# A longer pipeline for the attention sums of a graph network: four banks and buffers, totals two steps later, work moved between three engines

## The chip, the cores and the metric

The kernel runs on one core of one Trainium2 chip. The metric is the device time of one execution in microseconds (us); it comes from unprofiled runs. One more execution was profiled, and all rows below are from it. Engines are named as in the profile: PE is TensorE (PEld its weight loads), DVE VectorE, ACT ScalarE, POOL GpSimd, SP SyncE. A "q" behind an engine's name (SPq) marks work of its sequencer: register operations, waits, DMA issues.

## The reference, cut to what matters

A graph network of four layers over 6250 nodes and 100000 edges, whose targets `dst` are sorted. Layers 0 and 2 (heads H = 8 and 4) weigh the values of the edges by a softmax over each node's incoming edges and add them up. The core of it, from layer 0:

```python
a = jnp.exp(a - amax[edge_dst])
a = a / (jax.ops.segment_sum(a, edge_dst, num_segments=n)[edge_dst] + 1e-12)
ns = jax.ops.segment_sum(vs * a[..., None], edge_dst, num_segments=n).reshape(n, H * H0)
nv = jax.ops.segment_sum(vv * a[..., None, None], edge_dst, num_segments=n).reshape(n, H * H1, 3)
```

The kernel forms the sums of value times weight and the sums of the weights in one pass and divides later. One edge has 160 values: 64 scalars (`C0`), and 32 vectors in three components (`C1` = 32 columns each).

## The kernel before

The program is a row of phases with a barrier between them. `attention_sums` (L1339) is one of them and runs twice, for layer 0 and for layer 2. It walks over V = 244 blocks of 512 edges (128 partitions by `TM` = 4): 196 blocks of the sorted list, and up to 48 visited a second time, where a block spans two windows of 128 nodes. For each block:

- **SP** reads the block's number from `W["block"]` into a register (`value_load`) and issues three loads: values `val` (320 KB), targets `key`, weights `pb`. There are `RING` = 4 buffers of each. Before the load of block i it waits until block i-4 was weighed, by the semaphores `weighted_s` (DVE's part) and `weighted_v` (POOL's part).
- **POOL** adds the window's shift to the targets (`rel`), multiplies the three vector components of `val` by the weights into `wv`, and copies the weights themselves into the last H columns of `wv`.
- **DVE** multiplies the 64 scalar columns into `wv`, and compares `rel` with the lane numbers: `hot`, a 128 by 512 one-hot matrix of 0 and 1.
- **PE** adds up the block's edges by target: four matmuls of `hot` with `wv` into the PSUM bank `psS`, 160 + H columns wide. A matmul in f32 shows as two records, so a block has eight.
- **DVE** adds the bank to the running `total` (times `keep`, which is 0 where a new window begins), and **ACT** issues its store to `sums`.

`rel`, `hot`, `wv` and `psS` have two buffers each. `steps` (L84) writes a loop with a skew: in step n an engine works on block n for skew 0 and on block n-1 for skew 1. It unrolls the first steps (`lead`), then runs a hardware loop whose turn holds four steps, then the rest. `wait_apart` is a wait on a semaphore that is a separate instruction of the engine's sequencer; inside the loop the same instruction also counts up a spare semaphore.

Nothing orders the engines but these semaphores: each engine runs its own instructions in the order written.

Of the kernel before, what the change touches and what calls it, by code (L numbers as in the profile page):

```python
# [16 lines left out]
I32 = mybir.dt.int32  # L17
# [1321 lines left out]
def attention_sums(nc, W, D, layer, H, tag):  # L1339
    HS, HV = C0 // H, C1 // H  # L1340
    width = CX + H
    sums = D["sums"][layer]
    with ExitStack() as ctx:
# [5 lines left out]
        rel, hot, wv = ring("rel", [P, TM], 2, I32), ring("hot", [P, TM, P], 2), ring("wv", [P, TM, width], 2)  # L1349
        total = ring("total", [P, width], RING)  # L1350
        psS = [S.ps(f"psS{u}", [P, 512]) for u in range(2)]
        values, weights = blocks_of(D["val"]), blocks_of(D["probs"][H])
        targets = D["dst_sorted"].rearrange("p t -> (p t)").rearrange("(m q k) -> m q k", q=P, k=TM)
        LAST = 1
        block = ctx.enter_context(nc.Block())

        @block.sync
        def _(sp):
            sp.dma_start(sums[0], W["zeros"][:, 0:width]).then_inc(sem("first"), 16)

# [14 lines left out]
        def _(pool):  # L1375
            tt = nc.gpsimd.tensor_tensor

            def body(i_of):
                if m := i_of(0):
                    i, u, j = m  # L1380
                    wait_apart(pool, sem(f"in{u}"), (j + 1) * 48, sem("pool_passed"))
                    wait_apart(pool, sem("hot"), i - 1, sem("pool_passed"))
                    tt(rel[u % 2][:, :], key[u][:, :], W["shift"][:, bass.ds(i, 1)].to_broadcast([P, TM]), ALU.add).then_inc(sem("rel"), 1)
# [10 lines left out]
        def _(dve):  # L1394
# [3 lines left out]
            def body(i_of):  # L1398
                if m := i_of(0):
                    i, u, j = m  # L1400
                    dve.wait_ge(sem(f"in{u}"), (j + 1) * 48)
                    wait(dve, sem("summed"), i - 1)
                    tt(wv[u % 2][:, :, 0:C0].rearrange("p t (h c) -> p t h c", h=H), val[u][:, :, 0:C0].rearrange("p t (h c) -> p t h c", h=H),
                       bcast(pb[u][:, :, :], 3, HS), ALU.mult).then_inc(sem("weighted_s"), 1)
                    dve.wait_ge(sem("rel"), i + 1)
                    tt(hot[u % 2][:, :, :], bcast(W["lane"][:, :], 1, TM), bcast(rel[u % 2][:, :], 2, P), ALU.is_equal).then_inc(sem("hot"), 1)
# [1277 lines left out]
```

## Time and profile before

| | |
|---|---|
| median of 3 unprofiled runs | 12669.28 us (12666.13 to 12681.18) |
| the profiled execution | 12702.04 us, its span 12700.3 us |
| `attention_sums`, layer 0: SP's first load to its last | 2983.7 to 3603.5 us of the span |
| `attention_sums`, layer 2 | 9926.4 to 10530.4 us of the span |

The two phases are about a tenth of the span. No other phase contains a line that the change touches. The page gives for each engine the busy time and the share of the span; they are averages over phases of quite different kinds, and what the change is worth has to be read inside the two stretches of the table.

### The profile page before, as it was taken

Reading aid. Unit: us, or ns where it says so; the run is one execution under the profiler, and the core shown is the slowest. Engines: PE = TensorE matmul, PEld = TensorE weight load, DVE = VectorE, ACT = ScalarE, POOL = GpSimd, SP = SyncE. Lnnn points to the kernel's source line nnn. Section 1 sums busy time; section 2 is a strip of 40 time slices with the busy share of each in tenths; the row PEclk is TensorE's granted clock in tenths of the full one; section 3 lists DMA queues with packets and bytes.
Section 4 is the critical chain, followed back from the end, with each engine's and each line's share of the span. In section 5 each row is a group of like instructions: output and inputs, shape, how many; then the busy total and the mean of one; then the engine's idle time right before and its main releaser. Section 6 shows DMA issues by size and latency. Waiting matters only on the chain. (4 is left out here: it accounts for less than half of the span.)

```text
span 12700.3 us, 220425 instructions
## 1 busy us (share of the span) xinstructions
PE 9229.7 (73%) x44798; PEld 7244.6 (57%) x44798; DVE 8713.2 (69%) x21701; ACT 4529.6 (36%) x11637; POOL 8172.7 (64%) x8692
## 2 busy tenths in 40 slices
PE   2899999973655666666664578888887465999985
PEld 2888888863545322222223477777776454565654
DVE  4677777777643555555554389999999764667763
ACT  1455555540012222222221267777776001333331
POOL 4788888864843788888882176666664582666650
PEclk7777777776865777777776589999898786899995
DMA  3455555434620688888885233333332562333331
GB/s 91 106 114 115 113 113 114 115 85 112 170 74 15 111 131 131 131 130 131 130 132 141 102 79 81 81 81 81 81 81 67 129 170 59 84 87 87 93 87 41
DMA packets 1339110, 1293.91 MB, mean 102 GB/s; under 512 B 504078, under 2 KB 1142018, under 8 KB 1338374
## 3 DMA queue, kind: packets, MB, share of 16 engines
q0 software_dynamic: 347904, 594.12, 25.6%
q1 hardware_dynamic: 913580, 653.03, 20.0%
q10 hardware_dynamic: 77530, 45.68, 1.2%
q8 instruction: 36, 0.59, 0.0%
q14 instruction: 60, 0.49, 0.0%
HBM read 781.38 MB, written 510.73 MB: 102 GB/s over the span
## 5 line engine op out<-in xcount | busy, mean ns | idle before, releaser
L664 POOL DMA_INDIRECT e_gs<-tab_src,e_ix x1568 | 1708.1, 1089 | 763.2 <-issue 429.9
L664 POOL DMA_INDIRECT e_gd<-tab_dst,e_ix x1568 | 1610.7, 1027 | 477.8 <-issue 474.4
L715 PE MATMUL e_psS<-e_rows,e_same 128*128 128x480 f32 x1568 | 1113.6, 876 | 848.2 <-DVE e_same L689 848.2
L603 PE MATMUL e_psF<-w_ident,e_F 128*128 128x128 f32 x6272 | 1293.0, 315 | 246.9 <-ACT e_F L1822 233.0
L733 POOL DMA_INDIRECT acc<-e_sums,e_row x784 | 1247.5, 1591 | 239.0 <-issue 206.7
L715 PEld LDWEIGHTS e_psS<-e_rows,e_same 128*128 128x128 f32 x1568 | 430.6, 293 | 1541.7 <-issue 1514.7
L1642 POOL DMA_INDIRECT e_g<-tab_src,e_er x976 | 970.1, 994 | 525.1 <-issue 284.1
L633 ACT ACTIVATE e_FT<-e_psF 128x384 f32<-128x384 f32 (+1 forms) x2352 | 1078.0, 458 | 538.5 <-PE e_psF L603 526.4
L1431 PE MATMUL s_psS<-s_wv,s_hot 128*128 128x168 f32 (+1 forms) x3904 | 800.0, 361 | 615.2 <-POOL s_wv L1389 242.6
L603 PEld LDWEIGHTS e_psF<-w_ident,e_F 128*128 128x128 f32 x6272 | 895.5, 170 | 389.9 <-issue 346.0
L1431 PEld LDWEIGHTS s_psS<-s_wv,s_hot 128*128 128x128 f32 x3904 | 694.3, 228 | 720.4 <-issue 529.5
L664 POOL DMA_INDIRECT e_g<-tab_src,e_ix x784 | 834.0, 1064 | 248.3 <-issue 178.5
L723 ACT ACTIVATE e_sums<-e_psS 128x480 f32<-128x480 f32 x784 | 447.8, 571 | 1504.6 <-PE e_psS L715 1504.2
L613 PE MATMUL e_psO<-w_l_t,e_FT 128*128 128x160 f32 (+1 forms) x3136 | 892.9, 373 | 1.2 <-issue 0.9
L639 ACT ACTIVATE e_O<-e_psO 128x352 f32<-128x352 f32 (+1 forms) x1568 | 755.8, 482 | 364.5 <-PE e_psO L615 358.2
L2143 POOL TENSOR_TENSOR n_st<-n_st,w_half 128x8 f32<-128x8 f32 x70 | 113.4, 1638 | 1091.9 <-DVE n_st L2568 945.1
L1666 PE MATMUL e_psS<-e_rows,e_hot 128*128 128x384 f32 x1952 | 778.6, 549 | 37.8 <-issue 35.7
L1387 POOL TENSOR_TENSOR s_wv<-s_val,s_pb 128x128 f32<-128x128 f32 x1464 | 770.3, 553 | 38.2 <-PE s_psS L1431 37.2
L1554 DVE TENSOR_TENSOR e_prod<-e_g,e_dirs 128x384 f32<-128x384 f32 x196 | 109.6, 559 | 898.0 <-DMA e_g<-tab_src,e_ix 898.0
L615 PE MATMUL e_psO<-w_l_t,e_FT 96*128 96x96 f32 x3136 | 715.9, 316 | 0.0
L614 PEld LDWEIGHTS e_psO<-w_l_t,e_FT 128*128 128x128 f32 x3136 | 666.0, 234 | 0.0
L614 PE MATMUL e_psO<-w_l_t,e_FT 128*128 128x96 f32 x3136 | 663.7, 300 | 0.0
(471 smaller groups left out, 23529.8 us busy)
## 6 DMA issues: line engine op xcount, KB each, us to landing
s_val<-val SPq DMA_DIRECT2D x488, 320.0 KB
val<-e_O SPq DMA_DIRECT2D x392, 320.0 KB, 2.7
acc<-w_zeros SPq DMA_DIRECT2D x392, 139.5 KB
n_ag<-acc SPq DMA_DIRECT2D x56, 960.0 KB
e_krow<-in_src_t SPq DMA_DIRECT2D x196, 256.0 KB
sums<-e_total SPq DMA_DIRECT2D x244, 192.0 KB
e_es<-in_es SPq DMA_DIRECT2D x196, 130.0 KB
e_gs<-tab_src,e_ix POOLq DMA_INDIRECT x1568
```

The costliest lines, as they stand in the source:

```text
L603: last = nc.tensor.transpose(psF[:, P * g:P * g + P], F[:, k, P * g:P * g + P], ident[:, :])
L613: nc.tensor.matmul(o[:, 0:first], f[:, 0:P], W[w + "_t0"][:, :], start=True, stop=True, skip_group_check=True)
L614: nc.tensor.matmul(o[:, first:second], f[:, P:2 * P], W[w + "_t1"][:, :], start=True, stop=True, skip_group_check=True)
L633: nc.scalar.activation(FT[:, k, :], psF[:, 0:width], ACT.Copy).then_inc(S.sem(tag + "_FT"), 1)
L639: nc.scalar.activation(O[:, k, :], o[:, 0:width], ACT.Copy).then_inc(S.sem(tag + "_O"), 1)
L664: pool.indirect_dma_start(into[t][u][:, k, :], None, tables[t], bass.IndirectOffsetOnAxis(ix[u][:, t, k:k + 1], 0))\
L715: nc.tensor.matmul(psS[(k) % len(psS)], T["same"][u][:, k, :], values[:, k, :], start=True, stop=True)\
L733: pool.indirect_dma_start(acc[k], bass.IndirectOffsetOnAxis(T["row"][u][:, k:k + 1], 0), T["sums"][u][:, k, :], None, compute_op=ALU.add). ...
L1387: tt(wv[u % 2][:, :, a:a + C1].rearrange("p t (h c) -> p t h c", h=H), val[u][:, :, a:a + C1].rearrange("p t (h c) -> p t h c", h=H), bcas ...
L1431: last = nc.tensor.matmul(psS[u % 2][:, 0:width], hot[u % 2][:, k, :], wv[u % 2][:, k, :], start=(k == 0), stop=(k == TM - 1))
L1642: pool.indirect_dma_start(g[u][:, k, :], None, D["tab_src"], bass.IndirectOffsetOnAxis(er[u][:, k, 12:13].bitcast(I32), 0))\
L1666: last = nc.tensor.matmul(psS[u % 2][:, 0:width], hot[u % 2][:, k, :], rows[u % 2][:, k, :], start=(k == 0), stop=(k == TM - 1))
```

## The change

The banks `psS` and the buffers of `rel`, `hot` and `wv` go from two to four. DVE's totals and ACT's stores move from skew 1 to skew 3 (`TOTAL`), so that in its own order DVE prepares three blocks ahead of the one it totals; PE's sums get skew 1 (`SUM`), which on PE, that does nothing else here, changes only where steps are unrolled. ACT copies the weights into `wv` and has a semaphore of its own for it, `shares`; POOL keeps two of its three products, and DVE takes the third (the last component). PE waits for five semaphores instead of four, SP for three instead of two. With a skew of 3 the unrolled lead grows from four steps to eight.

```diff
-        rel, hot, wv = ring("rel", [P, TM], 2, I32), ring("hot", [P, TM, P], 2), ring("wv", [P, TM, width], 2)
+        rel, hot, wv = ring("rel", [P, TM], RING, I32), ring("hot", [P, TM, P], RING), ring("wv", [P, TM, width], RING)
-        psS = [S.ps(f"psS{u}", [P, 512]) for u in range(2)]
+        psS = [S.ps(f"psS{u}", [P, 512]) for u in range(RING)]
-        LAST = 1
+        SUM, TOTAL, LAST = 1, 3, 3
+        def weigh(tt, u, a, n):
+            heads = lambda t: t[u][:, :, a:a + n].rearrange("p t (h c) -> p t h c", h=H)
+            return tt(heads(wv), heads(val), bcast(pb[u][:, :, :], 3, n // H), ALU.mult)
...
@@ SP @@
                     wait_apart(sp, sem("weighted_s"), i - RING + 1, sem("sp_passed"))
                     wait_apart(sp, sem("weighted_v"), i - RING + 1, sem("sp_passed"))
+                    wait_apart(sp, sem("shares"), i - RING + 1, sem("sp_passed"))
...
@@ POOL @@
-                    wait_apart(pool, sem("summed"), i - 1, sem("pool_passed"))
-                    for d in range(3):
-                        a = C0 + C1 * d
-                        tt(wv[u % 2][:, :, a:a + C1].rearrange("p t (h c) -> p t h c", h=H),
-                           val[u][:, :, a:a + C1].rearrange("p t (h c) -> p t h c", h=H), bcast(pb[u][:, :, :], 3, HV), ALU.mult)
-                    nc.gpsimd.tensor_copy(wv[u % 2][:, :, CX:width], pb[u][:, :, :]).then_inc(sem("weighted_v"), 1)
+                    wait_apart(pool, sem("summed"), i - RING + 1, sem("pool_passed"))
+                    for d in range(2):
+                        last = weigh(tt, u, C0 + C1 * d, C1)
+                    last.then_inc(sem("weighted_v"), 1)
...
@@ DVE @@
+                    weigh(tt, u, 0, C0)
+                    weigh(tt, u, C0 + 2 * C1, C1).then_inc(sem("weighted_s"), 1)
...
-                if m := i_of(1):
+                if m := i_of(TOTAL):
...
@@ PE @@
-                if m := i_of(0):
+                if m := i_of(SUM):
...
+                    wait_apart(pe, sem("shares"), i + 1, passed)
-                    wait_apart(pe, sem("totals"), i - 1, passed)
+                    wait_apart(pe, sem("totals"), i - RING + 1, passed)
...
@@ ACT @@
-                if m := i_of(1):
+                if m := i_of(0):
+                    i, u, j = m
+                    wait_apart(act, sem(f"in{u}"), (j + 1) * 48, sem("act_passed"))
+                    wait_apart(act, sem("summed"), i - RING + 1, sem("act_passed"))
+                    nc.scalar.activation(wv[u][:, :, CX:width], pb[u][:, :, :], ACT.Copy).then_inc(sem("shares"), 1)
+                if m := i_of(TOTAL):
```

How the change moves instructions is seen in the loops. First SP, one of the four steps of a turn in layer 0, before. The bracket lists the semaphores waited for; a semaphore's number is used again from phase to phase, and the listing gives the name that it had first, so two names in the bracket are two waits (here `weighted_s` and `weighted_v`). "ISA" is a register operation or an assertion:

```order
L1366 ISA [waits setup_loaded,setup_wiped]
L1366 TENSOR_LOAD w_block
L1366 ISA x2
L1367 ISA
L1367 DMA s0_val0<-val 128x640
L1368 ISA
L1368 DMA s0_key0<-dst_sorted 128x4
L1369 ISA
L1369 DMA s0_pb0<-probs_8 128x32
```

The same step of the changed kernel:

```order
L1370 ISA [waits setup_loaded,setup_wiped,setup_shaped_dve]
L1370 TENSOR_LOAD w_block
L1370 ISA x2
L1371 ISA
L1371 DMA s0_val0<-val 128x640
L1372 ISA
L1372 DMA s0_key0<-dst_sorted 128x4
L1373 ISA
L1373 DMA s0_pb0<-probs_8 128x32
```

All that SP did it still does, in the same order; one wait more stands ahead of the block number's load.

Then DVE, one step of the turn in layer 0, before: the product of the block, its one-hot matrix, and the total of the block before it.

```order
L1403 TENSOR_TENSOR s0_wv1<-s0_val1,s0_pb1 128x4x64
L1405 REGISTER_ALU
L1406 TENSOR_TENSOR s0_hot1<-w_lane,s0_rel1 128x512
L72 REGISTER_ALU
L1413 ISA
L1413 SCALAR_TENSOR_TENSOR s0_total0<-s0_total3,w_keep,s0_psS0 128x168
```

The same step of the changed kernel:

```order
L1358 TENSOR_TENSOR s0_wv1<-s0_val1,s0_pb1 128x4x64
L1358 TENSOR_TENSOR s0_wv1<-s0_val1,s0_pb1 128x4x32
L1407 REGISTER_ALU
L1408 TENSOR_TENSOR s0_hot1<-w_lane,s0_rel1 128x512
L1411 REGISTER_ALU
L1415 ISA
L1415 SCALAR_TENSOR_TENSOR s0_total2<-s0_total1,w_keep,s0_psS2 128x168
```

DVE has one product more, and the total behind block 1's one-hot matrix is now that of the block three back (bank 2) instead of one back (bank 0).

## Rows read from the trace of the kernel before

**Rows 1.** Busy time of each engine in both phases: windows of the span

```profile
core 0: us, PE busy (x) PEld busy (x) DVE busy (x) ACT busy (x) POOL busy (x), PEclk, DMA share, GB/s
2990.00:3600.00 610.00, 401.34 (x1919) 348.65 (x1918) 399.09 (x718) 0.00 (x0) 487.17 (x1197) 0.86 0.64 170
9940.00:10530.00 590.00, 377.91 (x1898) 327.62 (x1896) 391.14 (x713) 0.00 (x0) 476.89 (x1188) 0.88 0.68 170
```

**Rows 2.** Who waited for whom, 2990 to 3590 us: total, times, longest

```profile
DVE s_total L1413 <- PE s_psS L1431: 166.9, 176, 2.5
...
POOL s_rel L1383 <- DMA s_pb<-probs: 88.2, 144, 1.3
```

**Rows 3.** Timeline near the end of layer 0's phase: start, duration, what

```profile
3598.52 0.33 SPq L1369 DMA_DIRECT2D s_pb<-probs  x1
...
3601.17 0.43 DVE L1403 TENSOR_TENSOR s_wv<-s_val,s_pb 128x256 f32<-128x256 f32 x1 [0.53 <-DMA s_pb<-probs]
...
3603.47 0.33 SPq L1369 DMA_DIRECT2D s_pb<-probs  x1
```

**Rows 4.** SP's load of the values, first and last start, layers 0 and 2

```profile
L1367 SPq DMA_DIRECT2D s_val<-val x244: 332/338/355, 2983.7 to 3602.4; - x122
L1367 SPq DMA_DIRECT2D s_val<-val x244: 332/333/355, 9926.4 to 10529.4; - x122
```

**Rows 5.** Timeline of SP, one turn of layer 0's loop (loads of the values)

```profile
3199.87 0.34 SPq L1367 DMA_DIRECT2D s_val<-val  x1
...
3202.38 0.34 SPq L1367 DMA_DIRECT2D s_val<-val  x1
...
3204.74 0.34 SPq L1367 DMA_DIRECT2D s_val<-val  x1
...
3210.03 0.34 SPq L1367 DMA_DIRECT2D s_val<-val  x1
```

**Rows 6.** Timeline of SP, one turn of layer 2's loop (loads of the values)

```profile
10028.65 0.33 SPq L1367 DMA_DIRECT2D s_val<-val  x1
...
10038.56 0.33 SPq L1367 DMA_DIRECT2D s_val<-val  x1
```

**Rows 7.** Timeline of SP, unrolled steps at the start, without any wait

```profile
2985.89 0.34 SPq L1367 DMA_DIRECT2D s_val<-val  x1
...
2988.01 0.33 SPq L1367 DMA_DIRECT2D s_val<-val  x1
```

**Rows 8.** SP's waits in layer 0's loop: count, duration min/median/max ns

```profile
L79 SPq EVENT_SEMAPHORE  x478: 17/17/17, 2991.7 to 3599.0; - x160
```

**Rows 9.** Groups of instructions, 2990 to 3600 us: busy, mean ns, idle before

```profile
L1431 PE MATMUL s_psS<-s_wv,s_hot 128*128 128x168 f32 x1919 | 401.6, 366 | 208.5 <-DVE s_total L1413 96.5 <-DVE s_wv L1403 80.9 <-POOL s_wv L1389 25.6
L1387 POOL TENSOR_TENSOR s_wv<-s_val,s_pb 128x128 f32<-128x128 f32 x719 | 380.0, 555 | 21.1 <-PE s_psS L1431 20.9
L1406 DVE TENSOR_TENSOR s_hot<-w_lane,s_rel 128x512 f32<-128x512 int32 x240 | 212.6, 886 | 14.9 <-POOL s_rel L1383 0.3
L1403 DVE TENSOR_TENSOR s_wv<-s_val,s_pb 128x256 f32<-128x256 f32 x239 | 116.5, 487 | 20.2 <-DMA s_pb<-probs 16.7
L1413 DVE SCALAR_TENSOR_TENSOR s_total<-s_total,w_keep,s_psS 128x168 f32<-128x168 f32 x239 | 92.7, 388 | 175.8 <-PE s_psS L1431 168.7 <-issue 6.3
L1389 POOL COPY s_wv<-s_pb 128x32 f32<-128x32 f32 x239 | 73.8, 309 | 0.0
```

**Rows 10.** The last block of layer 0: from DVE's product to its total

```profile
3606.00 0.42 DVE L1403 TENSOR_TENSOR s_wv<-s_val,s_pb 128x256 f32<-128x256 f32 x1
...
3607.97 0.20 POOL L1389 COPY s_wv<-s_pb 128x32 f32<-128x32 f32 x1
...
3608.77 2.34 PE L1431 MATMUL s_psS<-s_wv,s_hot 128*128 128x168 f32 x8 [0.95 <-DVE s_total L1413]
3611.31 0.39 DVE L1413 SCALAR_TENSOR_TENSOR s_total<-s_total,w_keep,s_psS 128x168 f32<-128x168 f32 x1 [2.82 <-PE s_psS L1431]
```

**Rows 11.** The nearest small copy on ACT, from another phase

```profile
L1822 ACT ACTIVATE e_F<-e_F,e_y 128x64 f32<-128x64 f32 x784 | 278.7, 355 | 0.0
```

More of the change, by code:

```diff
@@ L1339, in attention_sums @@
 def attention_sums(nc, W, D, layer, H, tag):
-    HS, HV = C0 // H, C1 // H
     width = CX + H
@@ L1381, in body @@
                     wait_apart(pool, sem(f"in{u}"), (j + 1) * 48, sem("pool_passed"))
-                    wait_apart(pool, sem("hot"), i - 1, sem("pool_passed"))
-                    tt(rel[u % 2][:, :], key[u][:, :], W["shift"][:, bass.ds(i, 1)].to_broadcast([P, TM]), ALU.add).then_inc(sem("rel"), 1)
-                    wait_apart(pool, sem("summed"), i - 1, sem("pool_passed"))
-                    for d in range(3):
-                        a = C0 + C1 * d
-                        tt(wv[u % 2][:, :, a:a + C1].rearrange("p t (h c) -> p t h c", h=H),
-                           val[u][:, :, a:a + C1].rearrange("p t (h c) -> p t h c", h=H), bcast(pb[u][:, :, :], 3, HV), ALU.mult)
-                    nc.gpsimd.tensor_copy(wv[u % 2][:, :, CX:width], pb[u][:, :, :]).then_inc(sem("weighted_v"), 1)
+                    wait_apart(pool, sem("hot"), i - RING + 1, sem("pool_passed"))
+                    tt(rel[u][:, :], key[u][:, :], W["shift"][:, bass.ds(i, 1)].to_broadcast([P, TM]), ALU.add).then_inc(sem("rel"), 1)
+                    wait_apart(pool, sem("summed"), i - RING + 1, sem("pool_passed"))
+                    for d in range(2):
+                        last = weigh(tt, u, C0 + C1 * d, C1)
+                    last.then_inc(sem("weighted_v"), 1)
             steps(pool, V, LAST, body, RING)
@@ L1401, in body @@
                     dve.wait_ge(sem(f"in{u}"), (j + 1) * 48)
-                    wait(dve, sem("summed"), i - 1)
-                    tt(wv[u % 2][:, :, 0:C0].rearrange("p t (h c) -> p t h c", h=H), val[u][:, :, 0:C0].rearrange("p t (h c) -> p t h c", h=H),
-                       bcast(pb[u][:, :, :], 3, HS), ALU.mult).then_inc(sem("weighted_s"), 1)
+                    wait(dve, sem("summed"), i - RING + 1)
+                    weigh(tt, u, 0, C0)
+                    weigh(tt, u, C0 + 2 * C1, C1).then_inc(sem("weighted_s"), 1)
                     dve.wait_ge(sem("rel"), i + 1)
-                    tt(hot[u % 2][:, :, :], bcast(W["lane"][:, :], 1, TM), bcast(rel[u % 2][:, :], 2, P), ALU.is_equal).then_inc(sem("hot"), 1)
-                if m := i_of(1):
+                    tt(hot[u][:, :, :], bcast(W["lane"][:, :], 1, TM), bcast(rel[u][:, :], 2, P), ALU.is_equal).then_inc(sem("hot"), 1)
+                if m := i_of(TOTAL):
                     i, u, j = m
@@ L1413, in body @@
                     nc.vector.scalar_tensor_tensor(out=total[u][:, :], in0=total[(u - 1) % RING][:, :], scalar=W["keep"][:, bass.ds(i, 1)],
-                                                   in1=psS[u % 2][:, 0:width], op0=ALU.mult, op1=ALU.add).then_inc(sem("totals"), 1)
+                                                   in1=psS[u][:, 0:width], op0=ALU.mult, op1=ALU.add).then_inc(sem("totals"), 1)
             dve.wait_ge(sem("empty"), 1)
@@ L1428, in body @@
                     wait_apart(pe, sem("weighted_s"), i + 1, passed)
-                    wait_apart(pe, sem("totals"), i - 1, passed)
+                    wait_apart(pe, sem("shares"), i + 1, passed)
+                    wait_apart(pe, sem("totals"), i - RING + 1, passed)
                     for k in range(TM):
-                        last = nc.tensor.matmul(psS[u % 2][:, 0:width], hot[u % 2][:, k, :], wv[u % 2][:, k, :], start=(k == 0), stop=(k == TM - 1))
+                        last = nc.tensor.matmul(psS[u][:, 0:width], hot[u][:, k, :], wv[u][:, k, :], start=(k == 0), stop=(k == TM - 1))
                     last.then_inc(sem("summed"), 1)
```

## The prediction

> **What bounds the kernel now.** I read the busy time of both stretches first. POOL is the busiest engine with 487 of 610 us in layer 0's phase and 477 of 590 in layer 2's; DVE and PE have about two thirds, ACT computes nothing [rows 1]. By shares alone POOL would be the one to relieve, and the chain PE to total to PE looks like a lockstep: DVE's total waits 167 us in all for PE [rows 2]. But no engine is full. A phase with no full engine is paced by a loop of waits or by something that busy time does not count, so I looked next for who waits for memory. POOL's first instruction of a block waits 144 times, 88 us in all, for the load of the weights [rows 2]. That is odd: there are four buffers, and a load may be issued three blocks ahead.
>
> The timeline says how far ahead it really is. The weights of block 241 are issued at 3598.52, and DVE's product at 3601.17 has just waited 0.53 us for them: it starts 2.65 us after the issue, and only the loads of two blocks are issued behind these, the last at 3603.47 [rows 3]. So a load is issued about one block before it is used. The permission for it (block i-4 weighed) was given long before. SP isn't held up by the buffers; it is late by itself.
>
> Its own pace confirms this. 244 loads of the values go from 2983.7 to 3602.4 us in layer 0, that is 618.7/243 = 2.546 us a block, and from 9926.4 to 10529.4 in layer 2, 2.481 us a block [rows 4]. A turn of four steps takes 3210.03 - 3199.87 = 10.16 us in layer 0 [rows 5] and 9.91 us in layer 2 [rows 6], with the same steps inside (2.51, 2.36, ...), though PE's, DVE's and POOL's instructions take turns of very different patterns around them. An engine that waited for others would show their jitter. SP issues three DMAs of 0.33 us each, 1.0 us of 2.5; the rest is register work, the load of the block number and the waits' own instructions. None of it counts as busy, so no table of shares shows the bound. **Both phases, 604.0 + 619.8 us from SP's first to last load, run at the speed of SP's instruction stream.** What waits in the other engines (PE for totals, totals for PE) is the slack of engines that are faster than SP.
>
> **The change part by part, against the profiled execution's 12702.0 us.**
>
> *Four banks and buffers, totals two steps later.* They remove waits of DVE, PE and POOL on one another. These engines then wait for the loads instead, and SP, which issues the same loads in the same order, is no earlier. Worth 0 in the loop. The cover is SP's pace: without it, DVE would set it (below).
>
> *POOL's product to DVE, the copy to ACT.* The window of 610 us holds 240 blocks. POOL is busy 487/240 = 2.03 us a block [rows 1]; it loses one product (380.0/719 = 0.53) and the copy (73.8/239 = 0.31) [rows 9] and comes to 1.2 us. DVE has 0.886 + 0.487 + 0.388 = 1.76 us [rows 9]. Its new product, 128x128, is not in the trace. It costs at least half of the 128x256 product (0.24) and at most all of it (0.49), as work by column with some fixed part; I take 0.30. DVE comes to 2.06, at most 2.25 us. SP takes 2.48 to 2.55. Covered, 0. ACT's copy of 128x32: the nearest row is 0.355 us for 128x64 [rows 11], which with a DMA issue of 0.34 fits four times over. Behind the total's wait on ACT stands the next block's copy, but that total has been done a step when the next load lands. 0.
>
> *PE's fifth wait.* PE is busy 401.6/240 = 1.67 us a block [rows 9]. At the lower clock one block is 2.34 us at the worst [rows 10]; with some 0.1 us for one more wait it remains under SP's 2.55, and it has three blocks of slack now. 0.
>
> *SP's third wait* (`shares`). This is the one edit on the engine that sets the pace. The weights were copied long before, so it never stops; but it is one instruction more per block. Price: the instruction itself is 0.017 us [rows 8], the lower bound. The upper one comes from comparing a step without waits, 2988.01 - 2985.89 = 2.12 us [rows 7], with the loop's shortest step, 3204.74 - 3202.38 = 2.36 [rows 5]. The 0.24 us between them are two waits and one register operation: at most 0.12 for a wait, if the register operation were free, 0.08 if the three are alike. The register operation lasts a little longer than a wait, so I take 0.072. After the change 59 turns of four steps remain per phase: 2 x 236 x 0.072 = **+34.0 us**; by the bounds +8 to +57.
>
> *Eight unrolled steps instead of four.* Blocks 4 to 7 leave the loop, where they cost 2.51 us on average, and cost 2.12 plus about one wait, 2.2, since unrolled waits need no counting instruction: 2 x 4 x 0.3 = **-2.5 us**.
>
> *The tail.* After the last load DVE's product starts at 3606.00, POOL's copy ends at 3608.17, PE starts 0.60 us later and takes 2.34 us, and the total ends at 3611.70 [rows 10]. POOL is done 0.5 + 0.3 us sooner; then DVE's one-hot matrix ends last, at 3606.00 + 0.42 + 0.30 + 0.89 = 3607.6, about 0.6 us before the copy did. 2 x 0.6 = **-1.2 us**. The two totals held back fit into PE's 2.3 us.
>
> *Where SP's loop lies.* The same 65 instructions take 10.16 us a turn in layer 0 and 9.91 in layer 2 [rows 5, 6]. The work is equal, so 0.25 us a turn hang on where the code stands in SP's program. The change makes the code ahead of both loops longer and moves them. In the extreme, both loops are then of the quick kind (-0.25 x 59 = -15 us) or both of the slow kind (+15). I counted instructions in the two programs: in the kernel before, the SP loops that turn slowly (this one and three in other phases) are those that contain one of the instructions 80, 208, 336, ... (every 128th), the seven quick ones contain none. With the longer code, layer 0's loop (490 to 558) contains none and layer 2's (1096 to 1164) contains 1104. So the two would swap: **0**, with 15 us to either side if the rule, which is only read off eleven loops, does not hold.
>
> Sum: 34.0 - 2.5 - 1.2 + 0 = **+30 us**, 12702 to 12732 in a profiled execution. The unprofiled median is 33 us lower before, so 12669 + 30 = **12699 us**, +0.24%. A difference below 0.2% (25 us) is about what a measurement of this kernel can't tell from no change, and the forecast lies just above.
>
> **The rivals.**
>
> *A. The engines set the pace, and the lockstep goes.* If PE and DVE's two buffers were what paces the phases, three blocks of lead would let each run at its own sum: the slowest would be DVE at 2.06 to 2.25 us a block, and SP would drop towards it, at best to its own 2.19. That is 2.51 - 2.25 = 0.26 us, 488 x 0.26 = 127 us, for **12542 us**. For it: the waits of rows 2, and POOL's share. Against it: SP's constant step and the load issued one block ahead [rows 3, 5]; both would have to be read wrongly. 5%. The Trainium skill speaks for this rival: "Perfetto Trace Analysis", under "Matmuls", wants independent groups to rotate through different PSUM banks so that one's evacuation overlaps the next one's matmuls, and under "Optimization Strategy" it reads a gap that repeats as a sign of too few buffers. By that rule the gap between PE's blocks would shrink; here the gap ends when the next block has landed and been weighed.
>
> *B. The wait costs little, or the placement falls well.* At the lower bound of 0.017 us the sum is 8 - 4 = +4; with 0.072 and both loops quick it is 30 - 15 = +15 us. **12673 to 12684 us**, no difference. For it: only 17 ns are recorded, and SP's loops are quick in seven of eleven cases. Against: the comparison of steps says 0.07 to 0.08. 10%.
>
> *C. DVE becomes the bound.* It decides from 2.6 us a block. DVE and POOL disturb one another already: the product's mean is 487 ns where quick instances take 0.42 to 0.43 [rows 3, 9, 10]. If the new product costs 0.49 and each of DVE's four instructions is held by 0.15 more, DVE takes 2.85: 488 x 0.25 = 122 us over the forecast's pace, **12820 us**. Against it: POOL has fewer instructions to collide with. 5%. The Trainium skill ("SBUF — State Buffer", "SBUF: two separate sides") calls the port pair of the two an exclusive lock for a whole instruction, taken also by a DVE operation with two inputs from SBUF, which the new product is; the longer products are what one would see of it.
>
> **How the numbers follow.** The forecast (SP paces both phases, one more instruction per block) has 80%. Its own range is 12684 to 12714 us: the swap may fail by 15 us to either side. Of its 80, some 57 lie above +25 us, since the centre is at +30 and the swap is well founded, and 23 within. A: 5, faster. B: 10, within. C: 5, slower. Together: slower 62, within 33, faster 5. The range reaches down into B and leaves out A, C and the outer parts: 12674 to 12716.
>
> **What would show it.** Right: SP's step inside the loop grows by 0.07 us at every place (2.36 to 2.43), its loads still reach DVE about one block ahead, and DVE, POOL and PE still wait for loads or for one another; PE's waits for totals disappear and come back as waits for DVE's or POOL's part. A turn takes about 10.2 us in layer 0 and 10.45 in layer 2. Wrong: SP's steps vary or grow by more than 0.1; a load is issued three blocks ahead of its use, with SP waiting for `weighted_s` (C); or the phases get shorter (A). The other phases should be as long as before; a shift there would be an effect of moved code that I count as 0.

## The result, and the profile after

The changed kernel takes 12709.55 us (median of 8 runs, 12694.66 to 12728.31); the kernel before, run beside it on the same chip, takes 12667.8 us (8 runs, 12645.73 to 12693.68). The two medians are 42 us apart. The ratio is 1.0032, with a 95% interval of 1.0021 to 1.0043: the change costs about 41 us, between 27 and 54. The forecast was 12699 us, +30 us, range 12674 to 12716.

The profiled execution after took 12716.73 us (span 12714.9, mean granted clock 0.789), that of before 12702.04 (span 12700.3, 0.791). Two single executions differ by 15 us here and two medians by 42; the stretches outside the two phases vary by some 20 us from one profile to the next. I therefore read the sums of the phases from their own rows and not from the spans.

Busy time of each engine in both phases after, the same view as [rows 1]:

```profile
core 0: us, PE busy (x) PEld busy (x) DVE busy (x) ACT busy (x) POOL busy (x), PEclk, DMA share, GB/s
2990.00:3600.00 610.00, 395.99 (x1906) 341.02 (x1905) 420.34 (x951) 54.39 (x238) 346.31 (x714) 0.87 0.67 168
9920.00:10540.00 620.00, 409.15 (x1897) 356.43 (x1897) 415.33 (x947) 51.14 (x237) 342.42 (x713) 0.82 0.66 161
```

POOL has given away 29% of its work (487 to 346 us), DVE and ACT have taken it, and the bytes per second went down by a little. No engine is above 69% busy. SP's loads of the values, which answer to [rows 4]:

```profile
L1371 SPq DMA_DIRECT2D s_val<-val x244: 332/333/355, 2982.1 to 3603.9; - x122
...
L1371 SPq DMA_DIRECT2D s_val<-val x244: 332/333/357, 9913.7 to 10547.9; - x122
```

That is 621.8 us in layer 0 (2.559 a block) and 634.2 us in layer 2 (2.610 a block), where before had 618.7 and 603.0. From the first load to the last total the phases are 629.3 and 643.1 us long, before 628.0 and 611.9: **+32.5 us in the two phases**.

One turn of SP's loop in layer 0, which answers to [rows 5]:

```profile
3196.02 0.34 SPq L1371 DMA_DIRECT2D s_val<-val  x1
...
3198.57 0.33 SPq L1371 DMA_DIRECT2D s_val<-val  x1
...
3201.08 0.33 SPq L1371 DMA_DIRECT2D s_val<-val  x1
...
3203.50 0.33 SPq L1371 DMA_DIRECT2D s_val<-val  x1
...
3206.27 0.34 SPq L1371 DMA_DIRECT2D s_val<-val  x1
```

A turn takes 10.25 us here and 10.28 on the mean of blocks 40 to 200; all turns below are such means, and the kernel before has 10.18 and 9.92 in the two layers. The steps repeat as before (2.55, 2.51, 2.42, 2.77), and the shortest has grown from 2.36 to 2.42. In layer 2, which answers to [rows 6]:

```profile
10027.13 0.34 SPq L1371 DMA_DIRECT2D s_val<-val  x1
...
10037.65 0.34 SPq L1371 DMA_DIRECT2D s_val<-val  x1
```

10.52 us here, 10.48 on the mean. Layer 2 is now the slower one; before it was layer 0.

Who waited for whom, 2990 to 3590 us, which answers to [rows 2]:

```profile
ACT s_wv L1446 <- DMA s_pb<-probs: 505.2, 216, 3.1
...
POOL s_rel L1387 <- DMA s_pb<-probs: 242.4, 218, 1.8
PE s_psS L1434 <- DVE s_total L1415: 194.8, 164, 2.0
DVE s_wv L1358 <- DMA s_pb<-probs: 180.5, 230, 1.5
```

This is the change in one view. DVE's 167 us of waits for PE are gone. In their place DVE, ACT and POOL wait for the load of the weights in nearly every one of 238 blocks. The last loads show how early they come:

```profile
3604.90 0.33 SPq L1373 DMA_DIRECT2D s_pb<-probs  x1
...
3607.51 0.63 DVE L1358 TENSOR_TENSOR s_wv<-s_val,s_pb 128x256 f32<-128x256 f32 x2 [0.58 <-DMA s_pb<-probs]
...
3609.42 1.41 PE L1434 MATMUL s_psS<-s_wv,s_hot 128*128 128x168 f32 x8 [0.31 <-POOL s_wv L1358]
3611.00 0.39 DVE L1415 SCALAR_TENSOR_TENSOR s_total<-s_total,w_keep,s_psS 128x168 f32<-128x168 f32 x1 [0.54 <-PE s_psS L1434]
```

The weights of the last block are issued at 3604.90 and used at 3607.51, 2.61 us later, nearly as long as before (2.65 for block 241, [rows 3]). With four buffers, four banks and totals two steps behind the sums, the loads are still issued one block ahead of their use, because SP issues them no earlier. The groups of the phase (busy, mean ns, idle before), which answer to [rows 9]:

```profile
L1434 PE MATMUL s_psS<-s_wv,s_hot 128*128 128x168 f32 x1906 | 396.6, 363 | 214.0 <-DVE s_total L1415 197.4 <-issue 14.1 <-DVE s_wv L1358 1.0
...
L1358 POOL TENSOR_TENSOR s_wv<-s_val,s_pb 128x128 f32<-128x128 f32 x476 | 302.4, 654 | 0.0
L1408 DVE TENSOR_TENSOR s_hot<-w_lane,s_rel 128x512 f32<-128x512 int32 x238 | 212.4, 893 | 3.9
L1358 DVE TENSOR_TENSOR s_wv<-s_val,s_pb 128x256 f32<-128x256 f32 x238 | 101.2, 425 | 185.5 <-DMA s_pb<-probs 183.7 <-PE s_psS L1434 1.6
L1415 DVE SCALAR_TENSOR_TENSOR s_total<-s_total,w_keep,s_psS 128x168 f32<-128x168 f32 x237 | 89.1, 376 | 0.0
L1358 DVE TENSOR_TENSOR s_wv<-s_val,s_pb 128x128 f32<-128x128 f32 x238 | 70.6, 297 | 0.0
```

DVE's new product takes 0.297 us (0.30 was forecast) and DVE comes to 0.893 + 0.425 + 0.376 + 0.297 = 1.99 us a block. PE is idle for as long as before (214.0 us after, 208.5 before, [rows 9]): the gap between its blocks did not shrink.

### The profile page after: what moved, and what is told of

Read it like the earlier page. It is cut to its first block and busy times, and to the rows that moved or that the text cites. A ratio compares the mean times of both kernels' runs of the same rounds, so it can differ in the third digit from the quotient of the medians.

```text
span 12714.9 us, 223343 instructions
## 1 busy us (share of the span) xinstructions
PE 9268.6 (73%) x44798; PEld 7279.4 (57%) x44798; DVE 8759.7 (69%) x22189; ACT 4635.6 (36%) x12125; POOL 7878.6 (62%) x7716
## 5 line engine op out<-in xcount | busy, mean ns | idle before, releaser
L1434 PE MATMUL s_psS<-s_wv,s_hot 128*128 128x168 f32 (+1 forms) x3904 | 829.7, 370 | 618.0 <-DVE s_total L1415 389.6
L1387 POOL TENSOR_TENSOR s_rel<-s_key,w_shift 128x4 int32<-128x4 int32 x488 | 114.2, 234 | 950.4 <-DMA s_pb<-probs 899.4
```

Source lines behind the costliest of these rows:

```text
L1434: last = nc.tensor.matmul(psS[u][:, 0:width], hot[u][:, k, :], wv[u][:, k, :], start=(k == 0), stop=(k == TM - 1))
```

## The experiments

The twelve kernels ran in three groups of four, each group on one chip together with the kernel before. The first and the last group ran on chips on which the kernel before takes some 14% longer (14431.38 us and 14423.18). So what is compared across the groups is ratios, and turns of SP's loop, which are alike there. The middle four ran beside a before of 12667.9 us. Every experiment has one profile, and the turns and phases come from it.

### The wait alone, in the kernel before

One wait more on SP, on a semaphore that has been passed long since, and nothing else:

```diff
                     wait_apart(sp, sem("weighted_s"), i - RING + 1, sem("sp_passed"))
+                    wait_apart(sp, sem("weighted_s"), i - RING + 1, sem("sp_passed"))
                     wait_apart(sp, sem("weighted_v"), i - RING + 1, sem("sp_passed"))
```

> The kernel before with one satisfied wait more on SP per block (a second wait on weighted_s for block i-4), nothing else. Theory S (SP's instruction stream sets the pace of both phases, and a satisfied wait costs 0.072 us of it): 2 x 240 x 0.072 = +35 us over the kernel before, ratio 1.0027; SP's turn of four steps grows from 10.16 to 10.45 us in layer 0 and from 9.91 to 10.2 us in layer 2. Theory E (the engines' waits on one another set the pace, SP has slack): 0 us, SP's turn unchanged. Theory C (the cost after the change came from DVE's extra product or the fifth wait of PE, not from SP): 0 us too.

Measured: 14473.48 us, ratio 1.0025 (1.0012 to 1.0038). SP's loads of the values, to be laid beside [rows 4]:

```profile
L1368 SPq DMA_DIRECT2D s_val<-val x244: 332/333/355, 3268.7 to 3907.2; - x122
...
L1368 SPq DMA_DIRECT2D s_val<-val x244: 332/333/354, 11196.6 to 11819.1; - x122
```

That is 638.5 and 622.5 us, where the kernel before has 618.7 and 603.0. SP's turns are 10.54 us in layer 0 and 10.23 in layer 2, where the kernel before has 10.18 and 9.92: +0.36 and +0.31. In the traces of this kernel and of the changed one the distance from one wait's instruction on SP to the next is 0.071 us, in 480 and in 472 places. Four waits are then 0.28 us a turn; why the turns grew by 0.03 to 0.08 more was not shown. **This one line, without banks, buffers or moved products, makes the kernel slower by about as much as the whole change does** (the intervals of 1.0025 and 1.0032 overlap).

### One wait instead of three, in the changed kernel

```diff
-                    wait_apart(sp, sem("weighted_s"), i - RING + 1, sem("sp_passed"))
-                    wait_apart(sp, sem("weighted_v"), i - RING + 1, sem("sp_passed"))
-                    wait_apart(sp, sem("shares"), i - RING + 1, sem("sp_passed"))
+                    wait_apart(sp, sem("summed"), i - RING + 1, sem("sp_passed"))
```

> The changed kernel in which SP waits for one semaphore per block instead of three: summed for block i-4, which PE raises only after all three parts of that block were read. Theory S: two waits fewer, 2 x 236 x 2 x 0.072 = -68 us against the changed kernel, so 1.0032 - 0.0054 = ratio 0.998 to the kernel before (-27 us); a step of SP in the loop 2.42 us in layer 0; loads are still issued one block ahead. Theory E or C: as the changed kernel, ratio 1.003.

Measured: 14409.15 us, ratio 0.9983 (0.9969 to 0.9998). The turns fall from 10.28 and 10.48 to 9.78 and 10.04 us. Eight waits less are 8 x 0.071 = 0.57, which would give 9.71 and 9.91. The rest is told by SP's own waits in this trace, layer 0 and layer 2 (us, times, longest):

```profile
SPq L79 <- PE s_psS L1432: 4.9, 15, 0.6
...
SPq L79 <- PE s_psS L1432: 8.3, 19, 1.3
```

Over some 58 turns that is 0.08 and 0.14 us a turn. 9.78 - 0.08 = 9.70, and 10.04 - 0.14 = 9.90: here the price of a wait holds to 0.01 us a turn.

### The copy back on POOL, without `shares`

ACT's copy and its semaphore go, POOL copies behind its two products, SP has two waits again, PE four:

```diff
-                    wait_apart(sp, sem("shares"), i - RING + 1, sem("sp_passed"))
...
-                        last = weigh(tt, u, C0 + C1 * d, C1)
-                    last.then_inc(sem("weighted_v"), 1)
+                        weigh(tt, u, C0 + C1 * d, C1)
+                    nc.gpsimd.tensor_copy(wv[u][:, :, CX:width], pb[u][:, :, :]).then_inc(sem("weighted_v"), 1)
```

> The changed kernel with the copy of the weights back on POOL, so no semaphore shares: SP waits for two and PE for four semaphores again, ACT only stores; four banks and buffers, the totals two steps later and DVE's extra product stay. Theory S: -34 us against the changed kernel, about +5 us or ratio 1.000 to 1.001 against the kernel before: the banks, the skew and the moved product are worth nothing. Theory C: still +30 us or more, ratio 1.003. If banks and skew are worth something that the third wait hid: below 0.998.

Measured: 14439.17 us, ratio 1.0005 (0.9991 to 1.0018), turns 9.95 and 10.20 us. This edit takes away the third wait on SP, ACT's copy and PE's fifth wait together; the experiment on the wait alone says which of them was costly. With them gone and banks, buffers, later totals and DVE's product kept, no difference from before can be measured: all that is costly in the change is its third wait on SP.

### SP's loop moved by twelve instructions, layer 2

To test that a turn's length hangs on where the loop lies, twelve increments stand ahead of SP's loop in layer 2 (run once on their own, outside the loop). The loop's own instructions are unchanged:

```diff
+            for _ in range(12 if layer == 2 else 0):
+                sp.sem_inc(sem("sp_passed"), 1)
```

> The changed kernel with 12 semaphore increments on SP ahead of layer 2's phase, executed once; they move the phase's loop of SP by 12 instructions, from 1096-1164 to 1108-1176, so that it contains no instruction 1104 any more. If the place of the code decides (every 128th instruction from the 80th, inside a loop, costs its turn 0.25 us): layer 2's turn falls from 10.45 to about 10.2 us and SP's first to last load from 634 to 619 us, layer 0 stays at 622 us; in all -15 us, less than one run can tell, so the phase is read. If layer 2's slower turn had another cause (its data, its 4 heads): 634 us as before.

The whole program was executed once, at 14471.9 us, so only the turns are read. Layer 2's fell from 10.48 to 10.25 us, and layer 0's, which was not moved, stayed at 10.26 (10.28):

```profile
L1373 SPq DMA_DIRECT2D s_val<-val x244: 332/333/355, 3266.8 to 3887.7; - x122
...
L1373 SPq DMA_DIRECT2D s_val<-val x244: 332/333/355, 11190.1 to 11811.6; - x122
```

621.5 us from first to last load in layer 2, against 634.2 in the changed kernel: 12.7 us for twelve instructions that do nothing. Within a turn nearly all of it lies at one place: from the branch back to the next instruction it is 0.168 us in the quick loop and 0.248 in the slow one, and the next load of the block number with its check, a few instructions behind, takes 0.11 us longer. The two loops of all fourteen kernels of this study can be sorted in this way: the branch takes 0.17 us in sixteen of the 28 and 0.25 to 0.27 in twelve. Counted in the traces, with one constant per layer for instructions that a trace does not show, the prediction's rule of every 128th instruction puts all 28 on the right side. The period itself is less certain: with such a free constant, anything from 124 to 152 would sort them as well.

### Six waits instead of three

```diff
                     wait_apart(sp, sem("shares"), i - RING + 1, sem("sp_passed"))
+                    wait_apart(sp, sem("weighted_s"), i - RING + 1, sem("sp_passed"))
+                    wait_apart(sp, sem("weighted_v"), i - RING + 1, sem("sp_passed"))
+                    wait_apart(sp, sem("shares"), i - RING + 1, sem("sp_passed"))
```

> The changed kernel with each of SP's three waits written twice: three satisfied waits more per block. Theory S: 2 x 236 x 3 x 0.072 = +102 us against the changed kernel, less 15 us because layer 2's loop then lies at 1124-1204 and holds neither instruction 1104 nor 1232: SP's turn 11.1 us in both layers (from 10.28 and 10.47), +128 us against the kernel before, ratio 1.009 to 1.010. Theory E: SP has slack, the turns stay.

Measured: 12783.71 us, ratio 1.0083 (1.0064 to 1.0101), a little below what was expected. Turns 11.04 us in both layers; phases 676.0 and 676.8 us, together 80 us longer than in the changed kernel, where 3 x 0.071 x 472 = 101 is the price. The longer loop also moved layer 2's to a quick place (its branch takes 0.168 us again), worth 13 us by the experiment above. That leaves 88, so the price is a little too high here: six waits in a row lie 0.069 us apart, and in layer 0, which stayed quick, twelve waits more lengthened the turn by 0.76 us, 0.064 each. On an engine with slack these waits would leave the phases as they are.

### The load of the targets on ACT

Three kernels take one of SP's three loads away and let ACT issue it, with the load of the block number that it needs. ACT's store of the total follows later, so that it doesn't hold up the next load. In the changed kernel:

```diff
-                    sp.dma_start(key[u][:, :], block_at(targets, at)).then_inc(sem(f"in{u}"), 16)
...
+                    wait_apart(act, sem("weighted_v"), i - RING + 1, sem("act_passed"))
+                    at = act.value_load(W["block"][0:1, bass.ds(i, 1)], min_val=0, max_val=NM - 1)
+                    act.dma_start(key[u][:, :], block_at(targets, at)).then_inc(sem(f"in{u}"), 16)
+                if m := i_of(2):
...
-                if m := i_of(TOTAL):
+                if m := i_of(5):
```

(the copy at step 2, the store at step 5). In the kernel before the same, with the store at step 3. The third is the changed kernel with, besides, the single wait of above.

> The kernel before with the load of the targets (key) issued by ACT instead of SP; ACT's stores move to skew 3, so that its loads run ahead; buffers, banks, totals and products as before. SP saves 0.515 us per block and could go at 1.97 us. Theory S: the phases get faster until the next bound. With two banks and two buffers that bound should be POOL (2.03 us busy and 0.3 to 0.4 between copy and next block) with PE's and DVE's lockstep, 2.3 to 2.4 us a block: -60 to -100 us, ratio 0.993 to 0.996. Theory E (the lockstep of two buffers paces it already): 0 us.

> The changed kernel with the load of the targets issued by ACT: ACT loads for block n, copies for block n-2, stores block n-5. SP saves 0.515 us and could go at 2.05 us, DVE has 1.99 us of work, ACT's instructions come to about 2.1 us. Theory S: 2.1 to 2.2 us a block, -190 us against the kernel before, ratio 0.985 to 0.987, and well below the run with two banks: only now the four banks and the moved work are worth something (some 100 us). If banks and moved work are worth nothing at any pace: the same as the kernel before with the load on ACT.

> As the run before it, with SP waiting for summed of block i-4 alone instead of three semaphores: SP could go at 1.91 us. If SP is still what paces the run with the load on ACT, this one is 2 x 236 x 0.144 = 68 us faster. If DVE (1.99 us of work) or ACT (about 2.1 us) has become the bound, 0 to 30 us: ratio 0.983 to 0.986.

Measured, and the phases from first load to last total (1239.9 us together in the kernel before, 1272.4 in the changed one):

| kernel | us | ratio (interval) | turns, us | both phases |
|---|---|---|---|---|
| before, targets on ACT | 12678.92 | 1.0007 (0.9996 to 1.0019) | 9.66, 10.00 | 1204.9 |
| changed, targets on ACT | 12563.79 | 0.9911 (0.9895 to 0.9927) | 9.30, 9.35 | 1141.6 |
| changed, targets on ACT, one wait | 12549.11 | 0.9902 (0.9886 to 0.9917) | 9.24, 9.24 | 1134.0 |

The last two are clearly faster than both kernels, by less than expected, and the last is the best version of this study. What the other engines wait for in the third, 2990 to 3540 us:

```profile
PE s_psS L1431 <- ACT s_wv L1448: 169.4, 186, 1.6
...
DVE s_wv L1358 <- DMA s_key<-dst_sorted: 81.0, 157, 1.2
...
POOL s_rel L1384 <- DMA s_key<-dst_sorted: 58.0, 76, 1.4
```

Now PE waits for ACT's copy and the products wait for the targets, both of which stand in ACT's stream. That stream is the new bound. ACT's loads of the targets, one turn of its loop:

```profile
3301.30 0.34 ACTq L1443 DMA_DIRECT2D s_key<-dst_sorted  x1
...
3303.76 0.35 ACTq L1443 DMA_DIRECT2D s_key<-dst_sorted  x1
...
3306.08 0.35 ACTq L1443 DMA_DIRECT2D s_key<-dst_sorted  x1
...
3308.37 0.35 ACTq L1443 DMA_DIRECT2D s_key<-dst_sorted  x1
...
3310.51 0.34 ACTq L1443 DMA_DIRECT2D s_key<-dst_sorted  x1
```

The steps are 2.46, 2.32, 2.29 and 2.14 us and come again in the next turn (2.47, 2.32, 2.29). Between blocks 40 and 200 of the two changed kernels ACT's instructions follow one another without a pause: its waits hold it for less than 0.01 us a block in either layer, while SP now does wait (88 us in 530). ACT has no more work on data than 0.23 us a block; its other instructions (block number, two DMAs, the waits) are as invisible in busy time as SP's were.

The first of the three is a miss: its phases are 35 us shorter in the profile, but no gain was timed (+9 us, from -5 to +24). In its trace the targets land late in a quarter of the blocks (POOL waits for them 62 times, 40.7 us in all, from 2990 to 3560 us):

```profile
3306.35 0.36 ACTq L1446 DMA_DIRECT2D sums<-s_total  x1
...
3307.69 0.35 ACTq L1442 DMA_DIRECT2D s_key<-dst_sorted  x1
...
3310.35 0.46 POOL L1382 TENSOR_TENSOR s_rel<-s_key,w_shift 128x4 int32<-128x4 int32 x1 [0.42 <-DMA s_key<-dst_sorted]
```

ACT stores a total and only then issues the next targets, 1.34 us later, for which POOL still waits 0.42 us at 3310.35. Without the copy ACT's own instructions take less than a step, so it reaches the store early and is held there by the total, 0.33 us a block in layer 0 and 0.44 in layer 2; the load of the targets behind the store is held with it. My edit built a chain of its own. So this kernel doesn't tell what two banks allow, and its difference to the other two is not the worth of the change. Where the 35 us went in the timed runs stays open.

### The targets not loaded at all

The clean form of that question: the load goes from SP and to no other engine. The blocks after the first four of a layer compare with old targets, so the sums are those of other targets, and each engine's work in a block is the same. In both kernels:

```diff
-                    sp.dma_start(key[u][:, :], block_at(targets, at)).then_inc(sem(f"in{u}"), 16)
+                    if isinstance(i, int) and i < RING:
+                        sp.dma_start(key[u][:, :], block_at(targets, at)).then_inc(sem(f"in{u}"), 16)
```

(the waits for `in` count two loads in place of three).

> The kernel before, with the loads of the targets (the key blocks) left out after the first four blocks of a layer: later blocks compare with old targets, so the one-hot matrices and the sums are those of other targets, and the work of the engines in each block is the same. SP issues one load less a block. If SP's stream paces the kernel before (my account), a block falls from 2.55 and 2.48 us to the next bound: SP itself near 2.0, the engines with their two banks and buffers near 2.35 (POOL's 2.03 us of work and its waits). Expected 60 to 80 us less, a ratio of 0.994 to 0.995. If the engines' lockstep on two banks already paces before (rival A), the ratio stays at 1.000.

> The same omission in the changed kernel: the targets of blocks after the first four of a layer aren't loaded, so the sums are those of other targets. By my account SP falls to some 2.05 us a block and DVE's work is 1.99, so a block takes near 2.1 us: 190 to 200 us less than before, a ratio near 0.985. What it is below the kernel before with the same omission is what the four banks and the moved product are worth once SP doesn't pace. If DVE and POOL in fact paced the changed kernel (rival C), the ratio stays near 1.003.

Measured: the kernel before 14189.98 us, ratio **0.9839** (0.9816 to 0.9862), turns 8.34 and 8.23 us; the changed kernel 14202.73 us, ratio **0.9845** (0.9823 to 0.9866), turns 8.18 and 8.41. The first expectation was far off, the second right. With two banks and two buffers the kernel before goes at 2.07 us a block, not at 2.35. Its lockstep therefore costs nothing down to there, and four banks bring nothing that a measurement shows. The granted clock of this stretch is 1.00, where the kernel before had 0.86 [rows 1]; whether two banks would do at 2.07 us with slower matmuls too was not tested. What sets the 2.07 is in the windows of layer 0, before first, then changed:

```profile
3270.00:3760.00 490.00, 322.03 (x1869) 269.37 (x1870) 388.15 (x703) 0.00 (x0) 484.60 (x1171) 1.00 0.73 206
```

```profile
3280.00:3760.00 480.00, 327.35 (x1880) 275.69 (x1879) 413.21 (x938) 53.91 (x235) 341.40 (x706) 0.99 0.75 210
```

In the kernel before POOL is now busy 484.6 of 490 us: full. SP waits for it (layer 0, then layer 2):

```profile
SPq L79 <- POOL s_wv L1390: 10.8, 48, 0.3
...
SPq L79 <- POOL s_wv L1390: 27.4, 116, 0.8
```

In the changed kernel POOL is at 71% and SP waits for nobody. So the product and copy that were moved from POOL save 38 us of SP's waits, and the third wait takes 34 us: the two kernels come out equal, at 1029.7 and 1022.9 us for both phases.

### The copy on POOL and the targets on ACT

Meant as the best mix: ACT without its copy, SP with one wait.

```diff
...
-                    wait_apart(act, sem(f"in{u}"), (j + 1) * 48, sem("act_passed"))
-                    wait_apart(act, sem("summed"), i - RING + 1, sem("act_passed"))
-                    nc.scalar.activation(wv[u][:, :, CX:width], pb[u][:, :, :], ACT.Copy).then_inc(sem("shares"), 1)
+                    wait_apart(act, sem("weighted_v"), i - RING + 1, sem("act_passed"))
+                    at = act.value_load(W["block"][0:1, bass.ds(i, 1)], min_val=0, max_val=NM - 1)
+                    act.dma_start(key[u][:, :], block_at(targets, at)).then_inc(sem(f"in{u}"), 16)
                 if m := i_of(TOTAL):
```

> The changed kernel with the load of the targets issued by ACT, the copy of the weights given back to POOL, and SP waiting only for the sums of four steps ago. Where the key load on ACT was run with ACT also copying, ACT's stream ended last at 2.31 us a block. If that was ACT's bound, ACT now has about 0.46 us less: ACT near 1.85, POOL near 1.84 of work and its gaps, DVE 1.99, SP 1.91, so a block near 2.2 us: 150 to 170 us less than before, a ratio of 0.986 to 0.989. If the late landing of loads issued by ACT set the 2.31 us, the ratio stays at 0.990.

Measured: 15662.74 us, ratio 1.085 (1.0824 to 1.0875), turns 20.5 us: 5.1 us a block. The store was left at `TOTAL`, three steps behind. A step in the timeline:

```profile
3500.35 0.89 DVE L1405 TENSOR_TENSOR s_hot<-w_lane,s_rel 128x512 f32<-128x512 int32 x1
...
3501.17 0.38 DVE L1412 SCALAR_TENSOR_TENSOR s_total<-s_total,w_keep,s_psS 128x168 f32<-128x168 f32 x1
...
3501.77 0.36 ACTq L1446 DMA_DIRECT2D sums<-s_total  x1
...
3503.05 0.35 ACTq L1442 DMA_DIRECT2D s_key<-dst_sorted  x1
3504.99 0.64 DVE L1358 TENSOR_TENSOR s_wv<-s_val,s_pb 128x256 f32<-128x256 f32 x2 [3.45 <-PE s_psS L1430]
```

On DVE the total of block i-3 stands behind the one-hot matrix of block i; ACT's store waits for this total, and the targets of block i+1 stand behind the store. So they are requested only when block i has been compared: one load at a time, 3.8 us from the matrix to the next product, in a closed circle. ACT is held 3.1 us in every block by its wait for the total. The forecast of a gain missed, and the kernel says nothing on ACT's bound, which was to be tested; it shows what the order on a queue costs when a prefetch stands behind a result. In the two faster kernels above the store stood two steps later, and its total was done before ACT came to it.

### One wait in the kernel before

```diff
-                    wait_apart(sp, sem("weighted_s"), i - RING + 1, sem("sp_passed"))
-                    wait_apart(sp, sem("weighted_v"), i - RING + 1, sem("sp_passed"))
+                    wait_apart(sp, sem("summed"), i - RING + 1, sem("sp_passed"))
```

> The kernel before, with SP waiting for the sums of four steps ago alone, one wait instead of two. By my account the wait is worth 0.071 us a block: 2 x 236 x 0.071 = 33.5 us less, a ratio of 0.9972, turns of 9.88 and 9.63 us. If the engines' lockstep on two banks stands just below SP's pace, only part of that comes: a ratio of 0.998 to 1.000, with turns that do not shorten by 0.28 us.

Measured: 14443.2 us (12 runs), ratio 1.0000 (0.9984 to 1.0017), turns 10.01 and 10.14 us. No gain, though SP has one instruction less a block. Its waits, layer 0 and then layer 2:

```profile
SPq L79 <- PE s_psS L1430: 7.7, 20, 0.7
...
SPq L79 <- PE s_psS L1430: 29.8, 41, 1.4
```

Per turn 0.13 and 0.50 us. Without them the turns would be 9.88 and 9.64, and the price of a wait says 9.90 and 9.64 (10.18 and 9.92 less 0.28). The instruction was saved, and the saving was given back: the matmuls of block i-4 end later than its products, and with four input buffers they end so near to SP's turn that SP now really waits, 61 times in two layers. In the changed kernel the same edit costs SP 13.2 us of waits and not 37.5. The 24 us between them are 0.17% of the time, as is the difference of the two ratios (0.9983 and 1.0000), whose intervals overlap.

## Why the prediction was right

**What paces the phases.** SP's instruction stream, as predicted. One more passed wait slows the kernel before as the change does; one taken away (copy on POOL) brings it back; three more cost 80 us; one of three loads less gives 1.6% in either kernel. Rival A (lockstep on two banks) is refuted: those two banks run at 2.07 us a block when SP lets them, and in the kernel before itself, at its own clock, SP never waits for a buffer. The DMA engines do not set the pace either: they are 64% busy at 170 GB/s in the kernel before and 73% at 206 GB/s once one small load is gone. The gap on PE that the Trainium skill's rule on rotating banks ("Perfetto Trace Analysis", "Matmuls") would have shrunk kept its size, 214 us of 610: it ended with the next block's products, not with a free bank.

A part of that gap is PE's own waits. PE waits first for `weighted_v`, which mostly comes last; the others have been passed by then, but each still costs 0.151 us of PE's stream (the median of 710 distances in layer 0 after, of 611 before). From PE's first wait to the first weight load it is 0.53 us with four waits and 0.77 with five (medians). The prediction put the fifth at some 0.1 us and held it covered by SP, which it was.

**SP's third wait, +34.0 us.** The distance of two waits is 0.071 us where 0.072 was taken: 33.5 us. This is the term that carries the result. That it fits to half a microsecond is partly luck: the prediction shared out a difference of two steps among three instructions, though the trace of the kernel before has the distance itself, 0.073 us in 240 places. And read from the turns of the experiments, a wait is worth between 0.064 and 0.09 us.

**The placement, 0.** The turns were forecast at about 10.2 and 10.45 us and came at 10.28 and 10.48. Layer 0's loop turned quick and layer 2's slow, as the rule of every 128th instruction says, and moving layer 2's by twelve instructions made it quick. In the 58 turns from block 8 to block 240, which are in the loop in both kernels, SP needs 35.2 us more in the two layers together; the waits are 32.9 of that. The 2 us left were not foreseen. They go with a load of the block number that takes 0.04 to 0.05 us more a turn; no cause was shown.

**Unrolled steps and tail, -2.5 and -1.2.** Up to the load of block 8 SP is 1.2 us sooner in the two layers together. The term of -2.5 was mis-sized: it took blocks 4 to 7 to cost 2.2 us each once unrolled. They begin so (2.19 us), but single steps among them take 2.4 to 2.95, and the four take 9.90 and 10.49 us where they took 10.53 and 9.96 in the loop, 0.1 us less in all. The rest of the 1.2 comes from the blocks ahead of them. What delays the single steps was not shown. The tails are 7.5 and 8.8 us after the last load where they were 9.3 and 8.9, together -1.9.

**The terms at nothing.** DVE's product was 0.297 us (0.30), its sum 1.99 us (2.06), POOL 346/238 = 1.46 us a block and not 1.2: its remaining products take 654 ns in place of 555. The mean hides two kinds. In the kernel before a product takes 0.41 us where DVE does nothing beside it (54 of 718 in layer 0) and 0.86 where all that runs beside it is DVE's one-hot matrix (127). In the changed kernel both engines start on the same load: the first of POOL's two products takes 0.45 us, and the second, which lies beside the one-hot matrix in every block, 0.86. So the disturbance that rival C counted on DVE's side falls on POOL. It was covered by SP all the same. ACT's copy, 0.229 us, waits 505 us for data and holds nobody up. Rival C (DVE the bound) didn't come: with SP relieved DVE is at 413 of 480 us and still not full. Rival B (a cheap wait or a lucky placement) is refuted by the 0.071 us and by the swap.

**A sign that did not come as told.** I wrote that PE's waits for totals would disappear and come back as waits for DVE's or POOL's part. The profile still names DVE's total for 194.8 us. The total is not what PE waits for: its place is taken by the last event ahead of PE's start, the total of an older block, which DVE computes behind the one-hot matrix. What holds PE is the arrival of the next block, and then its own five waits; that DVE, POOL and ACT themselves wait for the load in nine blocks of ten says it without PE's label.

**The sum.** +30 forecast, +32.5 in the phases, +42 between the medians (27 to 54 by the ratio). The 9 us beyond the phases lie within the interval and within what the other stretches vary; no cause for them was shown.

## What to carry to other kernels

When no engine is full and buffers are free, look at the engine that issues the loads: how long before its use is a load issued, and are the steps of the issuing engine constant to 0.01 us? If so, its stream is the bound, busy time won't show it, and every instruction in its loop has a price, passed waits too (here 0.07 us each, 34 us in the 472 blocks of the two loops). Banks, buffers and moved work were worth nothing here while that stream was the longest. And a load handed to another engine lengthens that engine's stream: ACT became the bound at 2.31 us a block with 0.23 us of work on data.

Of two semaphores that allow the same buffer to be refilled, one is a single instruction but fires later: the saving holds only while it still fires ahead of the issuer's turn. And a load that is moved to another engine must not stand behind a result on that engine's queue: here the kernel whose store waits for a total of the same step took 8.5% more, and the one whose store came two steps later 1% less (ACT's copy of the weights differs between them too).

## What the hardware did that I had not expected

- A wait that is passed at once is recorded with 17 ns on SP and costs 71. On PE it is recorded with 51 and costs 151, so of several waits on PE the one that comes last in time is cheapest at the end of the list (an inference; no kernel here tried it).
- The turn of a loop on SP costs 0.23 to 0.27 us more or less by where the loop lies; twelve instructions ahead of it changed 634.2 into 621.5 us.
- POOL's 128x128 product takes 0.41 us alone and 0.86 beside DVE's one-hot matrix, that is 555 ns on average in the kernel before and 654 in the changed one.
- The kernel before takes 12668 us on one chip and 14431 on another, while a turn of SP's loop in layer 0, with the changed kernel's code, is 10.28 us on the first and 10.26 on the second.
